# A four-layer transformer on one core: last products by token, residual added by TensorE, normalisation tile by tile

## The reference, cut to what matters

```
x = ln(x + attn0(x))     # softmax(x QK x' / sqrt(128)) x VO, one head of width 128
x = ln(x + ffn0(x))      # silu(x w1 s1) * (x w2 s2); gelu(. h1 s) ; gelu(. h2 s) ; (. w3) * s3
x = ln(x + attn1(x))     # 16 heads of 64, 4 key/value heads, causal softmax, Wo
x = ln(x + ffn1(x))      # relu(x w_fc)^2 w_proj
x = ln(x + attn2(x))     # 16 heads of 64 with biases, a pruning mask of its own, W_proj and b_proj
x = ln(x + moe2(x))      # out = x + sum over 8 experts with two gates per token
x = ln(x + attn3(x))     # 16 heads; per token a causal softmax over its own 64 channels, Wo and bo
x = ln(x + moe3(x))      # 8 experts, one gate per token
```

## Time and profile before

| | |
|---|---|
| median of 3 runs | 3764.69 us (3761.5 to 3766.67) |
| the profiled execution | 3765.0 us, of which the span of instructions is 3763.4 us |
| busy: PE, DVE, ACT, POOL | 85%, 64%, 52%, 35% of the span |
| mean granted clock of TensorE | 0.964 of 2.4 GHz |
| one sequence, from x arriving to the next x | about 927 us |

### The profile page before, as it was taken

The page is one execution under the profiler, slowest core; times in us unless marked ns, Lnnn a source line. Parts: engine busy times, 40 slices in busy tenths (PEclk is TensorE's granted clock), DMA queues, the critical chain, the costliest instruction groups (busy, mean ns, idle before and its releaser), DMA issues. The chain is left out here.

```text
span 3763.4 us, 52030 instructions
## 1 busy us (share of the span) xinstructions
PE 3193.0 (85%) x19436; PEld 2178.2 (58%) x19436; DVE 2395.7 (64%) x4521; ACT 1966.7 (52%) x4372; POOL 1330.0 (35%) x1068
## 2 busy tenths in 40 slices
PE   4897998888788798888978879888897887988888
PEld 2554557776355546777535554677753555477774
DVE  3357379994246638999415653899931575399983
ACT  1436267773253527777225352877622544277762
POOL 0213056670021307666003120766500312086640
PEclk9998999999899999999989989999998999999999
DMA  3000100000200010000110001000011000100001
GB/s 127 1 1 1 46 14 1 1 1 24 67 1 1 1 53 7 1 1 1 59 32 1 1 1 59 1 1 1 1 59 32 1 1 1 59 1 1 1 1 62
DMA packets 69652, 68.38 MB, mean 18 GB/s; under 512 B 6491, under 2 KB 49907, under 8 KB 69254
## 3 DMA queue, kind: packets, MB, share of 16 engines
q1 hardware_dynamic: 60288, 56.15, 4.8%
q10 hardware_dynamic: 9094, 8.72, 0.7%
HBM read 63.81 MB, written 1.05 MB: 17 GB/s over the span
## 5 line engine op out<-in xcount | busy, mean ns | idle before, releaser
L1321 POOL TENSOR_TENSOR arena<-arena 128x1536 f32<-128x1536 f32 (+9 forms) x480 | 1021.7, 2160 | 415.6 <-DVE arena L1380 327.6
L1201 PE MATMUL psum<-ident,arena 128*128 128x128 f32 (+7 forms) x7168 | 863.8, 278 | 226.5 <-ACT arena L1297 210.1
L1201 PEld LDWEIGHTS psum<-ident,arena 128*128 128x128 f32 (+7 forms) x7168 | 782.8, 136 | 337.2 <-ACT arena L1297 273.6
L1287 ACT ACTIVATE arena<-arena 128x64 f32<-128x64 f32 (+7 forms) x2048 | 714.3, 498 | 140.8 <-PE psum L1210 140.8
L1380 DVE TENSOR_TENSOR arena<-arena,psum 128x1536 f32<-128x1536 f32 (+9 forms) x480 | 495.5, 1068 | 57.4 <-ACT arena L1297 49.7
L1366 DVE TENSOR_TENSOR arena<-arena,psum 128x1536 f32<-128x1536 f32 (+9 forms) x480 | 495.1, 1066 | 8.1 <-POOL arena L1321 6.2
L483 POOL TENSOR_TENSOR rstd<-veps,mhalf 128x4 f32<-128x4 f32 x32 | 32.4, 1012 | 1242.4 <-DVE veps L474 1242.4
L1297 ACT ACTIVATE arena<-arena 128x1536 f32<-128x1536 f32 (+2 forms) x288 | 409.4, 1429 | 117.1 <-DVE arena L1366 116.7
L774 POOL TENSOR_SCALAR arena<-arena 128x512 f32<-128x512 f32 (+3 forms) x512 | 264.5, 532 | 579.9 <-DVE arena L746 579.9
L703 ACT ACTIVATE arena<-arena 128x512 f32<-128x512 f32 (+3 forms) x512 | 282.8, 554 | 267.3 <-DVE arena L741 266.8
L660 PE MATMUL psum<-ident,arena 128*128 128x128 f32 x1280 | 194.8, 297 | 152.9 <-ACT arena L714 91.2
(11 more groups left out here) (209 smaller groups left out, 4105.4 us busy)
## 6 DMA issues: line engine op xcount, KB each, us to landing
stream<-in_L_ffn_W SPq DMA_DIRECT2D x160, 256.0 KB, 3.1
arena<-in_L_ffn_h_w SPq DMA_DIRECT2D x8, 1024.0 KB, 8.0
arena<-in_L_ffn_w_w SPq DMA_DIRECT2D x12, 256.0 KB, 4.5
arena<-in_L_ffn_h_w ACTq DMA_DIRECT2D x2, 1024.0 KB
wa<-in_L_attn_W_attn ACTq DMA_DIRECT2D x1, 1536.0 KB
wq<-in_L_attn_Wq ACTq DMA_DIRECT2D x2, 512.0 KB
wo<-in_L_attn_Wo ACTq DMA_DIRECT2D x2, 512.0 KB
x<-in_L_attn_x SPq DMA_DIRECT2D x4, 256.0 KB, 4.0
```

The source lines that it names most:

```text
L1201: last = nc.tensor.matmul(ps[ch.half][0:rows, to:to + P], buf[:, c:c + rows], ident[:], start=first, stop=False, is_transpose=True, skip_g ...
L1287: nc.scalar.activation(by_key[:, 0:HD - r, j], keys[:, h, 0:HD - r], ACT.Exp, bias=NB[:, j:j + 1], scale=Q3[tt % 2][:, j:j + 1]).then_inc( ...
L1321: last = nc.gpsimd.tensor_tensor(of_piece(D3[n % 5], piece), q, keys_on(K3[tt % 2], k, nk, w), ALU.mult)
```

## The change

- **Six last products by token.** In the first attention, the two feed-forward stages, both 16-head stages and the channel stage the weights take the moving side and the activations the stationary side, so the result has tokens on the partitions. An fp32 product of 128x512 becomes four of 128x128. In five of the six, TensorE adds the residual first, by a product of xT with the identity (add_x); the output biases of A2 and the channel stage come in by a product of one row. In the first attention DVE scales by the reciprocal of the softmax sum and adds x (attn_rows_dve), and the spread of those reciprocals by POOL and PE is gone. The scale s3 of ffn0 goes into w3 by one POOL instruction per sequence (ffn0_pool).
- **Normalisation by tiles.** For each tile: bn_stats, bn_aggr, then on POOL the addition of eps and the power, each on a 128x1 tile, then scaling on DVE, one transpose, and an ACT copy of 128x128. The two expert stages keep the DVE addition and the four transposes ahead of it (turn_dve, turn_pe); the last normalisation has no transposes behind it.
- **16-head tiles projected as they end.** heads_rows projects a query tile one step after its last group's values are done; the two PSUM buffers of the values are shared with it by an order worked out beforehand (bank, bank_free). ACT copies the result of the first three tiles into rT at the next step; their statistics and scaling run on DVE in the loop, the power on POOL. Only the last tile is left for the end.
- **Bias from the masking.** L736 multiplies by -1/8 and takes the minimum, which is the bias of the exponential; L741 and its wait are gone, and ACT waits for each unit.
- **Channel stage.** ACT copies the projected tile at chunk 7 (ROWS), DVE takes statistics at chunk 9 and scales at chunk 15, POOL takes the power at chunk 14; residual is gone.

The core of the diff:

```diff
-        def norm_dve(dve, j, f, done, value, scale=None, bias=None, twice=False):
-            ...
-                nc.vector.scalar_tensor_tensor(rT[:], f, by, xT[:], op, ALU.add).then_inc(n["res"], 1)
-            norm_rows(dve, j)
+        def stats_dve(dve, j, k, i, src):
+            n = nrm
+            nc.vector.bn_stats(stats[:, 6 * i:6 * i + 6], src).then_inc(n["stat"], 1)
+            dve.wait_ge(n["stat"], NT * j + k + 1)
+            nc.vector.bn_aggr(mv[:, 2 * i:2 * i + 2], stats[:, 6 * i:6 * i + 6]).then_inc(n["aggr"], 1)
+
+        def rstd_pool(pool, j, k, i):
+            n = nrm
+            pool.wait_ge(n["aggr"], NT * j + k + 1)
+            nc.gpsimd.tensor_scalar(veps[:, i:i + 1], mv[:, 2 * i + 1:2 * i + 2], EPS, 1.0, ALU.add, ALU.mult)\
+                .then_inc(n["veps"], 1)
+            pool.wait_ge(n["veps"], NT * j + k + 1)
+            nc.gpsimd.tensor_tensor(rstd[:, i:i + 1], veps[:, i:i + 1], mhalf[:, 0:1], ALU.pow).then_inc(n["rstd"], 1)
...
+        def norm_dve(dve, j, src, done):
+            for k in range(NT + 1):
+                if k < NT:
+                    done(k)
+                    stats_dve(dve, j, k, k, src[k])
+                if k > 0:
+                    scale_dve(dve, j, k - 1, k - 1, src[k - 1])
...
-            pe.wait_ge(s["OT"], A.ng)
+                for k in range(NT - 1):
+                    if t == A.step[k]:
+                        heads_rows(pe, A, k)
+            heads_rows(pe, A, NT - 1)
+            for k, i in enumerate(A.order):
+                if k == NT - 1:
+                    idle_work(4, 5)
+                back_pe(pe, A.stage, k, i, k % 2)
+            idle_work(4, 2)
+
+        def heads_rows(pe, A, k):
+            s, i = A.s, A.order[k]
+            bank = A.bank("rows", k)[:, 0:P]
+            A.bank_free(pe, "rows", k)
+            add_x(bank, i)
+            if A.bias_out is not None:
+                nc.tensor.matmul(bank, ones[0:1, :], A.bias_out, start=False, stop=False)
+            pe.wait_ge(s["OT"], max(b for b, g in enumerate(A.groups) if g.i == i) + 1)
             for p in range(NPAIR):
-                last = nc.tensor.matmul(psS[0], A.wo[:, p * P:(p + 1) * P], QA[:, p * T:(p + 1) * T],
-                                        start=p == 0, stop=p == NPAIR - 1)
+                last = nc.tensor.matmul(bank, QA[:, p * T + i * P:p * T + (i + 1) * P], of_tile(A.wo, p),
+                                        start=False, stop=p == NPAIR - 1)
             last.then_inc(s["proj"], 1)
...
                     g = A.groups[t]
-                    act.wait_ge(s["negmax"], t + 1)
                     for j in range(g.pairs):
                         for half in range(2):
+
                             pr, u = two(PRG[t % 4])[:, half, g.cols(j)], g.u0 + 2 * j + half
-                            nc.scalar.activation(pr, pr, ACT.Exp, bias=nb[:, u:u + 1], scale=HD ** -0.5,
+                            act.wait_ge(s["masked"], u + 1)
+                            nc.scalar.activation(pr, pr, ACT.Exp, bias=nb[:, u:u + 1], scale=-1.0,
                                                  accum_out=rsum[:, u:u + 1]).then_inc(s["probs"], 1)
...
-                                                           scale=1.0, scalar=-BIG, op0=ALU.add, op1=ALU.max,
-                                                           accum_out=mx[:, u:u + 1]).then_inc(s["masked"], 1)
-                    dve.wait_ge(s["masked"], g.end)
-                    nc.vector.tensor_scalar(nb[:, g.u0:g.end], mx[:, g.u0:g.end], -HD ** -0.5, None, ALU.mult)\
-                        .then_inc(s["negmax"], 1)
+                                                           scale=-HD ** -0.5, scalar=BIG, op0=ALU.add, op1=ALU.min,
+                                                           accum_out=nb[:, u:u + 1]).then_inc(s["masked"], 1)
...
-            pe.wait_ge(s["act"], 3 * NM)
+            for i in range(NT):
+                add_x(psR[i], i)
+            pe.wait_ge(s["w3"], 1)
             for k in range(NM):
-                last = nc.tensor.matmul(psO, w3_0[:, k * P:(k + 1) * P], HA[:, k * T:(k + 1) * T],
-                                        start=k == 0, stop=k == NM - 1)
-            last.then_inc(s["down"], 1)
+                pe.wait_ge(s["act"], 2 * NM + k + 1)
+                for i in range(NT):
+                    last = nc.tensor.matmul(psR[i], of_tile(HA[:, k * T:(k + 1) * T], i), of_tile(w3_0, k),
+                                            start=False, stop=k == NM - 1)
+                    if k == NM - 1:
+                        last.then_inc(s["down"], 1)
...
+                if c == ROWS and tt > 0:
+                    act.wait_ge(s["proj"], tt)
+                    nc.scalar.activation(of_tile(rT, tt - 1), scratch[:, 0:P], ACT.Copy).then_inc(s["rows"], 1)
...
-                    if c == RESIDUAL:
-                        residual(tt - 1)
+                    if c == STATS:
+                        dve.wait_ge(s["rows"], tt)
+                        stats_dve(dve, 6, tt - 1, tt - 1, of_tile(rT, tt - 1))
+                    if c == SCALE:
+                        scale_dve(dve, 6, tt - 1, tt - 1, of_tile(rT, tt - 1))
```

287 lines of the change are left out of this document (157 added, 130 removed).

## The result

The changed kernel takes **3670.51 us** (median of 4 runs, 3669.64 to 3671.37), the kernel before beside it 3765.68 (3761.5 to 3767.25): ratio 0.9749, interval 0.9732 to 0.9766, that is 95.2 us less. The prediction was 3669.0 in a range of 3621 to 3722, so it is right in sign, size and range. Its profiled execution has a span of 3668.5 us.

The account below looks back on a forecast made before the run. No engine bounds the whole; between stages a chain of small steps does. Savings at stage ends and in head loops, less channel-loop and expert-stage losses, sum to 24.0 us per sequence, 96 in four: 3765.0 becomes 3669 us, range 3621 to 3722.

Parts of the forecast that it names:

- The ends: Ends of A1, A2 and channel stage: one tile's chain, 4.89 us, replaces 13.35, 13.35 and 8.25; saves 8.46 twice, 3.4 once.
- P: POOL's eps, self-wait and power on one 128x1 tile: taken as 0.9 us, between 0.74 and 1.35.
- Rival B: POOL's power costs by instruction, 1.35 us a pair, so four-tile chains outlast those they replace; 3707 us, chance 0.16.
- The tilewise chain between stages: Normalisation by tiles: saves 1.1 us behind ffn0, 0 ffn1, 0.4 first attention; loses 0.7 and 1.0 behind the expert stages.
- H4: Four-tile normalisation chain between stages, POOL serial: 5.63 us, against 4.94 before.
- A1's loop: Earlier exponentials save 9.5 us a sequence, three inserted projections cost 6.4 with 0.4 hidden; saved 3.5.
- A2's loop: Dropping L741 saves 1.2 us, a shorter circle 2.4, earlier exponentials about 1.3 twice, against three insertions; saved 2.5 a sequence.
- one of them hidden: In A2, one of three inserted projections of 2.36 us each lies hidden behind DVE's pruning.
- rival D: PE's granted clock falls to half in the head loops, making the kernel slower than before; 3809 us, chance 0.04.
- The channel stage: Loop: DVE's freed wait becomes a wait for ACT; ACT's extra copy and DVE's scaling lose 0.7 us a tile, 2.1.
- Rival E: DVE's freed 3.28 us a tile reach the channel stage's end, 9 us a sequence; 3633 us, chance 0.14.
- rival C: Inserted projections stop the head loops, the shorter circle gives nothing net, 6 us a sequence lost; 3693 us, chance 0.1.

Follow-up runs that it names:

- pow4: Changed kernel with one DVE eps and one four-column POOL power in the five normalisations between stages, instead of a pair per tile; 3669.96 us.
- rows_end: Changed kernel with all four query tiles of A1 and A2 projected behind the loop, still by token, none inserted in it; 3659.43 us.
- warm: Changed kernel with nine idle products on PE in A2, in the wait ahead of the second tile's projection; 3656.73 us.
- dve_copy: Changed kernel with DVE instead of ACT copying the projected tile in the channel stage, so DVE waits for it again; 3671.24 us.
- mask_back: Changed kernel with the exponentials' bias again from one small DVE instruction per group, ACT waiting for the group; 3724.88 us.
- end_fill2: rows_end with 20 idle products in the first expert stage's routing, not 16, and 12, 26 and 6 at three A2 steps; 3660.57 us.
- best_c: end_fill2 with one four-column power in the normalisation behind the second expert stage alone; 3655.89 us.
- warm_idle: warm with 20 idle products instead of 16 in the first expert stage's routing; 3651.68 us.
- best_d: warm_idle with one four-column power in the normalisation behind the second expert stage alone; 3649.80 us.

## Why the prediction was right, and where its steps were off

- **The ends.** Right. A1 4.72, A2 4.71, channel 4.79 us, forecast 4.89 each. Before, A2's end was the same 13.35 us as A1's. The saving is 8.6 twice and 3.5 once.
- **P.** Forecast 0.9, measured 0.83 (0.19, the self-wait, and 0.55). The power is neither purely by column nor by instruction: 0.55 for one column and 1.01 for four. Rival B, 1.35, is out. (Its price was 34 us by the prediction's own count of 19 times 0.45 a sequence, not 38.) The Trainium skill (GPSIMD Engine Reference, section 3.1) prices by dispatch and element, by which I had made the 1.01 us fall on the instruction; the 0.55 disagrees with that reading.
- **The tilewise chain between stages.** H4 was 5.35 us where 5.63 was forecast, but the overlap was worth more than I gave it: ffn0 saved 1.5 for 1.1, ffn1 0.4 for 0, the first attention 0.9 for 0.4 (not clear of what that stage moves by itself), and the last expert stage lost 0.41 to its last scaling (77.27 against 76.86) and 0.06 with the step behind it, where 1.0 was reckoned. The sign of my comparison of the pair with one power of four was wrong where the tiles come one after another (pow4: +0.18, +0.19, and more at the first attention) and right only behind the second expert stage (-0.61), where all four tiles wait for one sum.
- **A1's loop.** Forecast -3.5, measured 12.00 less 8.63 = -3.4. Both parts were larger and cancelled. With nothing inserted (rows_end) the stage is 12.83 us shorter than before, 2.70 of it at the end, so the bias gives 10.1 us in the loop (forecast 9.5). The insertions then cost 10.1 - 3.4 = 6.7 (forecast 6.0, three times 2.12 less 0.4), and the groups' reciprocals set against those of rows_end show 2.2 for each of the three. So the loop hides nothing of them, and PE is its bound, as the 94% and the gapless 3.11 us say.
- **A2's loop, the mis-sized term.** Forecast -2.5, measured 4.65 less 8.64: **+4.0**. With nothing inserted the loop is 6.8 us shorter (7.61 for the stage, less 0.8 at its end: 12.56 against 13.35), close to the 1.2, 2.4 and twice 1.3 that I listed. The insertions therefore cost 6.8 + 4.0 = 10.8 us, where I counted two of 2.36 and 0.95 on DVE, 5.7. The table under warm divides the 10.8 in this sequence: 0.9 before any insertion, 2.8 for the first, 0.4 on the way, 5.3 for the second, 1.4 for the third. At full clock the second costs 1.4, so at full clock the three and what lies between come to 6.0, close to the 5.7: "one of them hidden" was not the miss, since the second and the third are each half hidden. The miss is the clock, which the term did not have: 3.9 us for the second insertion, and 0.9 at the fourth group. Besides, the parts I listed sum to 0.5 (1.5 without DVE's 0.95) and not to 2.5.
- **The clock, rival D.** I gave it 0.04 as a loss in the dense loops. In A1's loop the clock rose from 0.98 to 1.00, in A2, also denser (PE busy 84% for 79%), it fell from 0.93 to 0.90. warm shows that filling the wait of PE ahead of the insertion brings it back, and pow4 that the same wait unfilled sometimes leaves it at full; what decides between the two stays open. So of rival D the mechanism was there, in A2, at about 4.8 us in this sequence and not at 35. From the Trainium skill (TensorE: Matmul & The Clock Gate, Part 1) I had taken that denser loops lose no clock: the trace agrees for A1 and not for A2.
- **The channel stage.** Forecast +2.1 in the loop, measured -0.4 (-3.87 less the 3.46 at the end), and 0.0, +0.2 and -0.2 in the other sequences: the loop did not change. The step that failed is the 0.7 a tile for ACT's extra copy and DVE's scaling. The freed 2.93 us did turn into waits for ACT, 2.24 and 0.87, as reckoned, but the middle periods together are the 187.6 us of before, and the last tile is no longer. Why the two additions cost nothing was not tried. Rival E is out (no period is shorter by 3 us, dve_copy).
- **The insertions as rival C.** Its condition, the shorter circle giving nothing net, fails for A1 (10.1 won, 6.7 paid) and holds for A2 (6.8 won, 10.8 paid). For the two loops together it nearly holds: -3.4 and +4.0 in this sequence, -1.2 on the mean of four, where I forecast -6.0. C's 6 us a sequence were lost almost in full, and the total stayed at my figure because other terms gave them back.

A2 fell short by 6.35 us in this sequence; the channel stage gave 2.57 more than forecast and the other stages 2.6 in small parts, which leaves 1.2. Over the four sequences A2 fell short by 5.0, the channel stage gave 2.3 more, A1 0.5 and the rest 2.1, and the sum is 23.9 for 24.0. That the median came out within 1.5 us of the forecast is luck in this cancelling: the ends, P and A1 were right by their mechanism, A2's loop and the channel loop were not.

## What to carry to other kernels

Projecting a tile as soon as it ends is worth nothing by itself where PE bounds the loop: it moves work from the end into the loop at full price (A1: 2.2 us a tile in the loop, 2.0 at the end). Where PE has slack it can be half hidden (A2: 1.4 us for the second and the third tile, 2.6 each at the end), and the same insertion costs 5.3 where it meets the half clock. Price each insertion at the clock of the window it lands in, and look at the wait ahead of it; nine idle products in that wait were worth 13.8 us in all, some 10 of them when set against the mean of the unfilled kernels' A2. Count an idle product by the trace's time for one before using it, since a wait overfilled costs one for one.

## What the runs showed of the hardware that was not expected

- The clock behind the same waits of PE (1.00 and 0.87 us in the routing) fell to 0.62 and 0.53 in three sequences of warm and in one of the changed kernel (101.37 us against 99.72), and stayed at 1.00 in the others. In mask_back and dve_copy it stayed up in all eight sequences with nothing filled, in rows_end it fell in all four. What decides it wasn't settled; with the 1.00 us filled the stage was at 99.7 in all sixteen sequences of four kernels (end_fill2, best_c, warm_idle, best_d).
- Half clock can be free: in A2 without insertions, transposes of 1.97 and of 1.09 us in the stretch in which DVE prunes gave 138.07 and 138.31 us, and a stage clock of 0.95 and of 0.99 the same 138.1 to 138.3 us in all eight sequences. The half clock that cost 3.9 us lies in the stretch behind that one, where the changed kernel has a projection inserted; that stretch was never run at full clock without one.
- Stages whose code an edit didn't touch moved between kernels with the clock: the channel stage from 392.5 to 396.8 us, A2 from 139.3 to 141.2 within one execution of the changed kernel and from 136.1 to 139.9 within one of pow4. So single-stage differences below some 2 us need the stage's granted clock beside them.
- GpSimd's power took 550 ns for one column and 1010 ns for four: a straight line through the two is 0.40 us fixed and 0.15 a column.
